# Gate products in four groups of 32 output partitions, and one normalisation moved from VectorE to GpSimd, in a one-core decoder kernel

## The chip, the cores and the metric

The kernel runs on one core of a Trainium2 chip. Its time is the device time of one launch in microseconds (us). Three runs of the kernel before gave 1087.9, 1089.44 and 1091.88 us; their median, 1089.44 us, is what a change is held against.

Engines are named as in the profile: PE is TensorE (PEld its weight loads), DVE is VectorE, ACT is ScalarE, POOL is GpSimd, SP issues most DMAs. They run side by side and meet at semaphores.

## The reference

On x of 8 sequences x 256 tokens x 1024 features (2048 tokens, D = 1024), all in float32:

```
x = x + attn(layernorm(x))            # embedding to 128 features, 4 layers of long convolution and MLP, back to 1024
x = x + xattn(layernorm(x), ctx)      # see below
x = x + ffn(layernorm(x))             # 8 experts of 1024x1024, top 2 per token, softmax of the two gate logits
```

In `xattn` every (sequence, feature) keeps the tokens whose context value is among the largest 154 of 256 (`crucial`) and has the others as a second set. Of both sets the maximum and mean over the tokens go through a 7-tap convolution over the features, a normalisation over all of them and a sigmoid; this gate multiplies the features of the set. In `ffn` the logits are `layernorm(x) @ gate_w` with `gate_w` of 1024 x 8; they choose each token's two experts.

## The kernel before

Everything is in one program for one core, written engine by engine, with semaphores by hand; nothing is scheduled by a tool. X holds the tokens as 16 tiles of 128 tokens x 1024 features; T holds the same data turned, as 8 blocks of 128 features x 2048 tokens; M holds the mask of crucial tokens in bfloat16. The stages that matter here, with their places in the profiled execution:

- **Up to 376 us**: the 4 layers, and on the side the masks from the context.
- **Stage A, 376 to 464 us**: one step per tile t. PE adds the last product of the attention part (`products`, L243 to L246) for tile t + 3. DVE takes mean and variance of tile t (`ln_stats`, L226 to L231). POOL raises the variance to the power -1/2 (`ln_pow`, L235, one 128x1 instruction per tile). DVE writes the normalised tile, (x - mean) * rstd, into one of two buffers, `ring` (`normed`, L1806, a tensor_scalar of 128x1024). PE turns it (L1569), ACT copies it into T and sums it (L1701). Three tiles later DVE multiplies T with the mask and takes the maximum (`crucial`, L1789, four instructions of 128x256 per tile), one tile after that it takes the rest and its maximum (`maxima`, L1798, four as well); ACT sums the crucial part (L1710). DVE's own program gives the order: statistics of t, `crucial` of t - 3, `normed` of t, `maxima` of t - 4.
- **Gate products, first part.** The logits are linear in x, so the part of normalised x is taken from T ahead of the gating: `first_part(c, first, last)` (L1333) multiplies gate_w with 512 tokens, 8 products of 128x8 weights and 512 columns for each of 4 chunks c, all summed into partitions 0 to 7 of one bank. PE does five halves (4 products each) behind the last tiles of stage A, two halves in stage B, the last one in stage C.
- **Stage B, 464 to 477 us**: the convolution on PE (L1590 to L1595), and a chain between DVE, PE, POOL and ACT for the normalisation and the sigmoid. PE fills its waits with `keep_busy` (L1603), six dense bfloat16 products each time, whose results nobody reads.
- **Stage C, 477 to 530 us**: one step per sequence b. DVE and POOL multiply T by the gate (`gated_half`, L1472), PE turns it back (L1621), DVE adds it to X (L1877) and takes new statistics. `second_part` (L1640) multiplies gate_w with the gated T: 8 products with 256 columns per sequence. The 8-partition sums are copied by DVE (L1897, L1905) and turned by PE (L1628, L1647: transposes of 8 partitions).
- **530 to 564 us**: DVE routes the tokens. **From 564 us**: the experts, 37 tiles of 16 products each, PE alone (L2099).

Of the kernel before, what the change touches and what calls it, by code (L numbers as in the profile page):

```python
# [31 lines left out]
def crucial_count(c):  # L32
    f = int(LAMBDA * c // 1)
    return f + f % 2


def decoder_kernel(nc, x, ctx_map, w_in, b_in, ln1_w, ln1_b, phz_re, phz_im, lc_re, lc_im, sc_lin, ln2_w, ln2_b,
# [33 lines left out]
    with ctx:  # L71
# [3 lines left out]
        def sem(name):  # L75
            return ctx.enter_context(nc.semaphore(name))
# [21 lines left out]
        wout_t, bout_b = late[:, 0:D], late[:, D:2 * D]  # L98
        gate = sb("gate", [P, KD, E])
        convw = sb("convw", [P, 2 * TAPS])  # L100
# [47 lines left out]
        ld_misc = sem("ld_misc")  # L148
        ld_gate = sem("ld_gate")
        const_ready = sem("const_ready")  # L150
        set_pe = sem("set_pe")
# [230 lines left out]
        with nc.Block() as block:  # L382
            @block.sync
            def _(sp):
# [49 lines left out]
                context(3)  # L434
                sp.dma_start(gate[:, :, :], gate_w.rearrange("(k p) e -> p k e", p=P)).then_inc(ld_gate, 16)
                weights(2)
# [12 lines left out]
            def _(pool):  # L449
# [73 lines left out]
                def last_threshold(b):  # L523
# [784 lines left out]
        pooled = ewide[:, 0:4 * KD * B].rearrange("p (m i k b) -> p m i k b", m=2, i=2, k=KD)  # L1308
        logits = sb("logits", [P, NT, E])
        totals = logits[:, :, :].rearrange("p t e -> p (t e)")[:, 0:KD * B].rearrange("p (k b) -> p k b", k=KD)  # L1310
# [12 lines left out]
        def pool_at(i, n):  # L1323
            b, h = divmod(n, CT)
            return pooled[:, 0, i, h * KU:(h + 1) * KU, b]

        def first_part(pe, c, first, last):

            if first == 0:
                pe.wait_ge(t_set, (c + 1) * KD * GROUP // S)  # L1330
                pe.wait_ge(x1_done, 2 * (NT - 2) + c + 1)
            for k in range(first, last):
                mm = nc.tensor.matmul(bank[P1_SUMS[c]][0:E, :], gate[:, k, :], T[:, k, c * GROUP:(c + 1) * GROUP], start=(k == 0), stop=(k == KD - 1))  # L1333
            if last == KD:
                mm.then_inc(p1_mm, 1)
# [22 lines left out]
        std = in_late(NT)  # L1358
        g_part = in_late(E)
        known = in_late(NT, E)  # L1360
        shift = in_late(NT, E)
# [95 lines left out]
        P1 = N // GROUP  # L1457
        by_expert = [fin[0:E, u, :] for u in range(2)]

# [29 lines left out]
        col_s = [sb(f"col_s{u}", [P, QK], U32) for u in range(IN_FLIGHT)]  # L1489
        col_d = [sb(f"col_d{u}", [P, 1], U32) for u in range(IN_FLIGHT)]  # L1490
        col_p = [sb(f"col_p{u}", [P, 1]) for u in range(IN_FLIGHT)]
        xg_in = [sem(f"xg_in{u}") for u in range(IN_FLIGHT)]
# [10 lines left out]
        with nc.Block() as block:  # L1503
# [22 lines left out]
            def _(pool):  # L1526
                for t in range(CT, NT):
                    ln_pow(pool, 0, t)

# [30 lines left out]
            def _(pe):  # L1560
# [63 lines left out]
                def first_turned(c):  # L1624
                    pe.wait_ge(p1_cp, c + 1)
                    for u in range(GROUP // P):
                        t = c * (GROUP // P) + u
                        mm = nc.tensor.transpose(bank[P1_BANK][:, t * E:(t + 1) * E], by_expert[c % 2][:, u * P:(u + 1) * P], ident[0:E, 0:E])  # L1628
                    mm.then_inc(p1_tp, 1)

                def second_part(b):
# [7 lines left out]
                    for k in range(KD):  # L1639
                        mm = nc.tensor.matmul(bank[P2_SUMS[b % 2]][0:E, 0:S], gate[:, k, :], T[:, k, b * S:(b + 1) * S], start=(k == 0), stop=(k == KD - 1))  # L1640
                    mm.then_inc(p1_mm, 1)

                def second_turned(b):
                    pe.wait_ge(p1_cp, P1 + b + 1)
                    for h in range(CT):
                        t = CT * b + h
                        mm = nc.tensor.transpose(bank[P2_BANK][:, t * E:(t + 1) * E], by_expert[b % 2][:, h * P:(h + 1) * P], ident[0:E, 0:E])  # L1647
                    mm.then_inc(l_mm, 1)
# [131 lines left out]
            def _(dve):  # L1780
# [20 lines left out]

                def normed(t):
                    if t >= 2:
                        hold(dve, x1_tp, (t - 1) * KU)
                    dve.wait_ge(ln_rstd, t + 1)
                    v.tensor_scalar(ring[t % 2], X[:, t, :], mean_of(0, t), rstd_of(0, t), ALU.subtract, ALU.mult).then_inc(ln_out, 1)  # L1806

                for t in range(NT + LAG + 1):
# [40 lines left out]
                link(v.tensor_scalar(z[:, :, :], z[:, :, :], 0.0, None, ALU.max))  # L1849
                link(v.tensor_reduce(g_part, gate[:, :, :].rearrange("p k e -> p e k"), AX.X, ALU.add))  # L1850
                dve.wait_ge(g_act, 1)
# [41 lines left out]
                def first_sums(c):  # L1893
                    if c >= 2:
                        hold(dve, p1_tp, c - 1)
                    hold(dve, p1_mm, c + 1)
                    v.tensor_copy(by_expert[c % 2], bank[P1_SUMS[c]][0:E, :]).then_inc(p1_cp, 1)  # L1897

                def second_sums(b):
# [4 lines left out]
                    hold(dve, p1_mm, P1 + b + 1)  # L1904
                    v.tensor_copy(by_expert[b % 2][:, 0:S], bank[P2_SUMS[b % 2]][0:E, 0:S]).then_inc(p1_cp, 1)  # L1905

# [315 lines left out]
```

## Time and profile before

| | |
|---|---|
| runs | 1087.9, 1089.44, 1091.88 us; median 1089.44 |
| profiled execution | 1089.82 us, of which the span of the instructions is 1087.9 us |
| busy, whole span | PE 92%, DVE 50%, POOL 42%, ACT 35% |
| mean granted clock of PE | 0.955 of 2.4 GHz |
| L2099, the experts | 511.1 us of PE |
| L1333 and L1640, the gate products | 30.1 and 28.8 us of PE |

The span is what lies between the first and the last instruction of the program. A busy time is the union of the instructions of a group; a mean is over single ones. PE's records overlap, since a product starts while the one ahead of it drains: what a product costs in a series is the distance of two starts. PE writes two records for each float32 product (64 records for the 32 products of L1333). A number in square brackets behind a row is the idle time of that engine just ahead of it and what ended it. Idle time of an engine that others do not wait for costs nothing.

### The profile page before, as it was taken

To read this page: it belongs to the slowest core of one execution; us is meant where nothing else is said; L and a number is where in the kernel's file an instruction comes from. 1 tells how busy PE (TensorE), PEld (TensorE's weight loads), DVE (VectorE), ACT (ScalarE), POOL (GpSimd) and SP (SyncE) were. 2 spreads that over 40 slices of the span, in tenths; PEclk is the share of its full clock that TensorE was granted. 3 is DMA by queue.
4 is the path that set the end of the run, shared out by engine and by line. 5 is a ranking of instruction groups with operands and counts; after the bars stand their busy time and mean duration, and the time that the engine had idled before them with its cause. 6 is when DMAs were issued, how large, how long until landed. Compare 5 with 4: busy or idle time off the path is not lost. (4 is left out here: it accounts for less than half of the span.)

```text
span 1087.9 us, 13206 instructions
## 1 busy us (share of the span) xinstructions
PE 995.9 (92%) x3505; PEld 525.7 (48%) x3512; DVE 538.7 (50%) x1547; ACT 383.5 (35%) x1032; POOL 453.9 (42%) x567
## 2 busy tenths in 40 slices
PE   6888989999989799899469999999999999999995
PEld 5777555565555454245234444444444444444442
DVE  5645878999978889979952111111211111111111
ACT  2344868888865278668410000000000000000000
POOL 4823655665552010048244334333334444444441
PEclk9888989999989899899759999999999999999998
DMA  7320120110001330007758463737337364373332
GB/s 298 129 98 2 50 88 1 59 40 2 1 1 54 144 113 1 2 20 286 295 208 259 103 203 77 231 77 226 82 82 226 77 204 104 77 231 77 77 77 39
DMA packets 38461, 120.24 MB, mean 111 GB/s; under 512 B 6220, under 2 KB 9351, under 8 KB 38408
## 3 DMA queue, kind: packets, MB, share of 16 engines
q1 hardware_dynamic: 25592, 79.77, 19.8%
q0 software_dynamic: 12816, 39.86, 16.7%
q8 instruction: 21, 0.34, 0.1%
q14 instruction: 32, 0.26, 0.1%
HBM read 82.91 MB, written 36.70 MB: 110 GB/s over the span
## 5 line engine op out<-in xcount | busy, mean ns | idle before, releaser
L2099 PE MATMUL bank<-T,X 128*128 x1184 | 511.1, 595 | 3.7 <-issue 3.7
L2099 PEld LDWEIGHTS bank<-T,X 128*128 128x128 f32 x1184 | 225.9, 191 | 288.3 <-issue 288.3
L2144 DVE TENSOR_SCALAR X<-bank,col_p 128x512 f32<-128x512 f32 x37 | 27.8, 751 | 397.1 <-PE bank L2099 397.1
L2117 ACT ACTIVATE X<-bank,col_p 128x512 f32<-128x512 f32 x37 | 25.4, 687 | 495.8 <-PE bank L2099 469.7
L2062 POOL DMA_INDIRECT out_dram<-X,col_d x37 | 60.0, 1622 | 264.3 <-DVE X L2144 248.1
L2053 POOL DMA_INDIRECT X<-x_nrm,col_s x152 | 145.5, 957 | 50.8 <-issue 46.2
L850 ACT ACTIVATE M<-X,T 128x256 bf16<-128x256 f32 x152 | 75.0, 500 | 0.0
L490 POOL TENSOR_TENSOR rs<-ve,neg_half 128x4 f32<-128x4 f32 x36 | 43.7, 1214 | 57.9 <-DVE ve L978 57.9
L665 PE MATMUL bank<-nat,T 128*128 128x512 f32 x128 | 63.2, 614 | 2.5 <-ACT X L838 1.4
L1501 DVE STREAM_TRANSPOSE X<-X 128x1024 f32<-128x1024 f32 x39 | 48.4, 1240 | 26.3 <-DMA X<-x_nrm,col_s 12.7
L673 PE MATMUL bank<-X,T 128*128 128x512 f32 x128 | 60.6, 602 | 0.0
L607 PE MATMUL bank<-ident,rs 128*128 128x128 f32 x320 | 44.5, 285 | 16.4 <-POOL rs L490 14.2
L607 PEld LDWEIGHTS bank<-ident,rs 128*128 128x128 f32 x320 | 41.7, 195 | 36.5 <-POOL rs L490 23.0
L235 POOL TENSOR_TENSOR late<-late,neg_half 128x1 f32<-128x1 f32 x32 | 17.7, 556 | 93.3 <-DVE late L231 93.0
L838 ACT ACTIVATE X<-bank,T 128x512 f32<-128x512 f32 x64 | 43.5, 686 | 19.4 <-PE bank L665 17.9
L1009 DVE MAX8 T<-T 128x8 f32<-128x256 f32 x128 | 44.8, 412 | 0.1
L984 DVE TENSOR_TENSOR nat<-H,bank 128x512 f32<-128x512 f32 x36 | 24.5, 682 | 38.9 <-PE bank L607 38.5
L969 DVE TENSOR_TENSOR_SCAN X<-layer_par,X 128x256 f32<-128x256 f32 x64 | 42.7, 730 | 2.1 <-POOL X L494 2.0
L481 POOL TENSOR_TENSOR T<-T 128x8 f32<-128x8 f32 x88 | 38.2, 434 | 7.9 <-POOL T L481 1.4
L665 PEld LDWEIGHTS bank<-nat,T 128*128 128x128 f32 x128 | 21.7, 191 | 36.4 <-ACT X L838 21.8
L602 PEld LDWEIGHTS bank<-inv_col,nat 128*128 128x128 f32 x288 | 37.2, 202 | 2.6 <-ACT nat L825 2.2
L602 PE MATMUL bank<-inv_col,nat 128*128 128x1 f32 x288 | 37.1, 250 | 0.8 <-ACT nat L825 0.8
(341 smaller groups left out, 1426.6 us busy)
## 6 DMA issues: line engine op xcount, KB each, us to landing
T<-in_L_ffn_expert_w_dram SPq DMA_DIRECT2D x8, 4096.0 KB, 17.6
out_dram<-X SPq DMA_DIRECT2D x17, 512.0 KB
M<-in_x_dram SPq DMA_DIRECT2D x16, 512.0 KB, 7.2
X<-in_x_dram SPq DMA_DIRECT2D x16, 512.0 KB, 5.9
x_nrm<-H SPq DMA_DIRECT2D x16, 512.0 KB, 3.4
T<-in_ctx_dram SPq DMA_DIRECT2D x9, 512.0 KB, 3.7
X<-x_nrm,col_s POOLq DMA_INDIRECT x152
X<-in_ctx_dram SPq DMA_DIRECT2D x4, 512.0 KB, 7.0
```

The source lines that it names most:

```text
L490: g.tensor_tensor(rs[:, v % CH, :], ve[:, v % CH, :], neg_half[:, 0:TPC], ALU.pow).then_inc(done, 1)
L602: mm = nc.tensor.matmul(var_at(v, first)[:, i:i + 1], chunk(sq, v)[:, i * P:(i + 1) * P], inv_col[:, :], start=True, stop=True)
L607: mm = nc.tensor.matmul(bank[to][:, i * P:(i + 1) * P], rs[:, v % CH, i:i + 1].to_broadcast([P, P]), ident[:, :], start=True, stop=True)
L665: nc.tensor.matmul(bank[HD[t % 2]][:, :], w1s[v // CH % 2][:, t * P:(t + 1) * P], chunk(yn, v), start=True, stop=True).then_inc(hid_mm, 1)
L673: mm = nc.tensor.matmul(h_bank(v), w2c[v // CH % 2][:, t, :], hid[:, v % 2, t, :], start=False, stop=(t == FT - 1), skip_group_check=True)
L838: a.activation(hid[:, v % 2, t, :], bank[HD[t % 2]][:, :], ACT.Silu, bias=b1f[v // CH % 2][:, t:t + 1]).then_inc(hid_act, 1)
L850: a.activation(out_, tile_y(b, i), ACT.Sign, bias=at[b % 2][:, i:i + 1], accum_out=sums[b % 2][:, i:i + 1]).then_inc(done, 1)
L1009: v_.max(top16[b % 2][:, h * HT + i, r * 8:(r + 1) * 8], w[:, h, i, :]).then_inc(round_max, 1)
L1501: nc.vector.transpose(xgt_blocks[u], xg_blocks[u]).then_inc(xg_tp, 1)
L2053: g.indirect_dma_start(out=xg[u][:, c * QD:(c + 1) * QD], out_offset=None, in_=x_quarters, in_offset=bass.IndirectOffsetOnAxis(ap=col_s[u] ...
L2062: g.indirect_dma_start(out=out[:, :], out_offset=bass.IndirectOffsetOnAxis(ap=col_d[u][:, 0:1], axis=0), in_=yv[u], in_offset=None, comput ...
L2099: mm = nc.tensor.matmul(bank[2 * u + n][:, :], xgt[u][:, k, :], Tf[:, ds(odd * D + (k * N + n * BANK), BANK)], start=(k == 0), stop=(k == ...
```

## The change

- The weights `gate` get 32 columns per block instead of 8; POOL clears them first (one memset of 128x256 at the start of its program), and the DMA of gate_w, which now waits for that, fills columns 0 to 7.
- The 8 products of a sum no longer go to the same 8 partitions. Product k writes 32 partitions beginning at 32 * (k mod 4), so that the four groups each sum two products. The sums are copied by DVE with all 128 partitions.
- The transposes of the 8-partition sums become products with `sum_e`, a 128x8 matrix of ones and zeros that turns the sums and adds up the four groups at once. DVE makes `sum_e` from the identity with one tensor_reduce in stage B.
- `normed` leaves DVE's program and stands in POOL's, for every tile behind the power of that tile.
- `logits`, `col_d` and `col_p` get no memory of their own and share that of `center`, `mv` and `ve`, which are free by then.

```
+        gate = sb("gate", [P, KD, GROUP_E])                       # GROUPS = 4, GROUP_E = 32
+        sp.wait_ge(gate_clear, 1)
+        sp.dma_start(gate[:, :, 0:E], ...)
+        g.memset(gate[:, :, :], 0.0).then_inc(gate_clear, 1)
...
+        def of_group(sums, k):
+            j = k % GROUPS
+            return sums[j * GROUP_E:(j + 1) * GROUP_E, :]
...
-                mm = nc.tensor.matmul(bank[P1_SUMS[c]][0:E, :], gate[:, k, :], T[...], start=(k == 0), stop=(k == KD - 1))
+                mm = nc.tensor.matmul(of_group(bank[P1_SUMS[c]], k), gate[:, k, :], T[...], start=(k < GROUPS), stop=(k >= KD - GROUPS))
...
-        mm = nc.tensor.transpose(bank[P1_BANK][...], by_expert[c % 2][:, u * P:(u + 1) * P], ident[0:E, 0:E])
+        mm = nc.tensor.matmul(bank[P1_BANK][...], by_expert[c % 2][:, u * P:(u + 1) * P], sum_e[:, :], start=True, stop=True)
...
 POOL
-                for t in range(CT, NT):
-                    ln_pow(pool, 0, t)
+                def normed(t):
+                    if t >= 2:
+                        pool.wait_ge(x1_tp, (t - 1) * KU)
+                    pool.wait_ge(ln_rstd, t + 1)
+                    nc.gpsimd.tensor_scalar(ring[t % 2], X[:, t, :], mean_of(0, t), rstd_of(0, t), ALU.subtract, ALU.mult).then_inc(ln_out, 1)
+                for t in range(NT):
+                    if t >= CT:
+                        ln_pow(pool, 0, t)
+                    normed(t)
 DVE
-                    if t < NT:
-                        normed(t)
...
+                v.tensor_reduce(sum_e[:, :], ident[...].rearrange("p (j e) -> p e j", j=GROUPS)[:, 0:E, :], AX.X, ALU.add)
...
-                    v.tensor_copy(by_expert[c % 2], bank[P1_SUMS[c]][0:E, :]).then_inc(p1_cp, 1)
+                    v.tensor_copy(by_expert[c % 2], bank[P1_SUMS[c]][:, :]).then_inc(p1_cp, 1)
```

DVE's program in the middle of stage A, before: what stands between the last `crucial` instruction of a tile (the first row) and the first `maxima` instruction (ISA is how the program lists these two kinds; the rows with ewide alone read their result).

```order
L1789 ISA H,ewide<-T,M 128x256
L1789 ISA ewide 128x1
L1806 TENSOR_SCALAR nat<-X,late 128x1024
L1798 ISA fin,ewide<-T,H 128x256
L1798 ISA ewide 128x1
```

The same place of DVE's program now (the line numbers have moved by 21).

```order
L1810 ISA H,ewide<-T,M 128x256
L1810 ISA ewide 128x1
L1819 ISA fin,ewide<-T,H 128x256
L1819 ISA ewide 128x1
L1819 ISA fin,ewide<-T,H 128x256
```

One instruction per tile is gone there, and the eight of `crucial` and `maxima` stand in one row. POOL's program at the start of stage A, before (L235 is the power, x14 says how many stand in a row):

```order
L1525 UNCONDITIONAL_BRANCH
L235 TENSOR_TENSOR late<-late,neg_half 128x1 x14
L1531 TENSOR_TENSOR late<-late,neg_half 128x2
L1472 TENSOR_TENSOR T<-T,nat 128x4x256 x4
```

and now:

```order
L1538 UNCONDITIONAL_BRANCH
L1544 TENSOR_SCALAR nat<-X,late 128x1024 x2
L240 TENSOR_TENSOR late<-late,neg_half 128x1
L1544 TENSOR_SCALAR nat<-X,late 128x1024
L240 TENSOR_TENSOR late<-late,neg_half 128x1
```

The sixteen instructions of 128x1024 stand on POOL, each behind the power of its tile. On PE the order of the products is what it was; only their output partitions and, for 24 small ones, their kind differ.

## Rows read from the trace of the kernel before

**Rows 1.** The chain that ended last, in order of time: start, length, what
```profile
563.64 511.13 PE bank L2099 x1184
```

**Rows 2.** Busy time by stretch: length, each engine (instructions), clock, DMA share, GB/s
```profile
394.00:464.00 70.00, 63.48 (x215) 27.75 (x216) 65.11 (x283) 53.62 (x242) 5.40 (x10) 0.95 0.02 9
...
477.00:530.00 53.00, 50.77 (x299) 28.36 (x298) 48.34 (x124) 44.58 (x76) 42.05 (x35) 1.00 0.60 229
```

**Rows 3.** Timeline of DVE, one tile of stage A: start, length, instruction
```profile
410.66 0.43 DVE L1789 CUSTOM_DVE_ANT_0 H<-T,M 128x256 f32<-128x256 f32 x1 [0.23 <-ACT T L1701]
...
412.05 0.81 DVE L1806 TENSOR_SCALAR nat<-X,late 128x1024 f32<-128x1024 f32 x1
412.77 0.42 DVE L1798 CUSTOM_DVE_ANT_0 fin<-T,H 128x256 f32<-128x256 f32 x1
...
416.21 0.43 DVE L1789 CUSTOM_DVE_ANT_0 H<-T,M 128x256 f32<-128x256 f32 x1 [0.23 <-issue]
```

**Rows 4.** Timelines of DVE and PE: where the steady pace begins; PE's own pace
```profile
394.00 0.42 DVE L1789 CUSTOM_DVE_ANT_0 H<-T,M 128x256 f32<-128x256 f32 x1 [1.25 <-ACT late L1710]
413.68 1.13 PE L1569 MATMUL bank<-ident,nat 128*128 128x128 f32 x8
...
418.51 1.05 PE L1569 MATMUL bank<-ident,nat 128*128 128x128 f32 x8
```

**Rows 5.** Timeline of POOL: the power of a tile, beside DVE and alone
```profile
387.50 0.75 POOL L235 TENSOR_TENSOR late<-late,neg_half 128x1 f32<-128x1 f32 x1 [3.57 <-DVE late L231]
410.50 0.54 POOL L235 TENSOR_TENSOR late<-late,neg_half 128x1 f32<-128x1 f32 x1 [5.01 <-DVE late L231]
```

**Rows 6.** Timelines of POOL and DVE: L974 beside a long POOL instruction, and without
```profile
95.14 1.35 POOL L494 TENSOR_TENSOR X<-nat,T 128x512 f32<-128x512 f32 x1 [10.86 <-ACT nat L830]
95.28 1.76 DVE L974 TENSOR_TENSOR X<-X,T 128x512 f32<-128x512 f32 x1
260.61 0.68 DVE L974 TENSOR_TENSOR X<-X,T 128x512 f32<-128x512 f32 x1
```

**Rows 7.** POOL's groups by shape: names, shapes, count | busy, mean ns | idle before
```profile
L548 POOL TENSOR_SCALAR_AFFINE_SELECT upto_neg<-upto_neg 128x128 f32<-128x128 f32 x1 | 0.3, 286 | 0.0
L550 POOL TENSOR_SCALAR_AFFINE_SELECT ewide<-ewide 128x390 f32<-128x390 f32 x1 | 0.5, 501 | 0.0
L1472 POOL TENSOR_TENSOR T<-T,nat 128x1024 f32<-128x1024 f32 x14 | 32.8, 2363 | 6.0 <-ACT nat L1739 6.0
```

**Rows 8.** Timeline of PE, end of stage A and stage B
```profile
440.80 1.97 PE L1569 MATMUL bank<-ident,nat 128*128 128x128 f32 x8 [4.58 <-DVE nat L1806]
...
453.56 10.47 PE L1333 MATMUL bank<-T,gate 128*8 128x512 f32 x24
464.87 0.71 PE L1590 MATMUL bank<-ewide,band 128*128 128x128 f32 x4 [0.84 <-DVE ewide L1826]
...
467.15 1.46 PE L1603 MATMUL bank<-ones,ident 128*128 128x512 bf16 x6
...
470.34 7.03 PE L1333 MATMUL bank<-T,gate 128*8 128x512 f32 x16
```

**Rows 9.** Busy time by stretch around PE's pause of 4.58 us
```profile
436.00:439.00 3.00, 0.22 (x2) 0.00 (x0) 2.55 (x11) 1.21 (x7) 0.54 (x1) 1.00 0.00 0
442.00:445.00 3.00, 3.00 (x7) 0.74 (x6) 2.59 (x11) 3.00 (x17) 0.54 (x1) 0.50 0.01 3
448.00:464.00 16.00, 16.00 (x49) 4.41 (x48) 14.85 (x77) 10.69 (x49) 0.54 (x1) 1.00 0.01 2
```

**Rows 10.** Timeline of PE: keep_busy products ahead of the experts, at the low clock
```profile
549.97 1.87 PE L1603 MATMUL bank<-ones,ident 128*128 128x512 bf16 x4
```

**Rows 11.** Timelines of DVE and PE in stage C: sums of chunks 2, 3, of sequences 0, 1
```profile
484.41 1.28 DVE L1897 COPY fin<-bank 8x512 f32<-8x512 f32 x2
486.08 7.07 PE L1640 MATMUL bank<-T,gate 128*8 128x256 f32 x32
489.85 0.41 DVE L1905 COPY fin<-bank 8x256 f32<-8x256 f32 x1 [1.53 <-PE bank L1640]
```

More of the change, by code:

```diff
@@ L1332, in first_part @@
             for k in range(first, last):
-                mm = nc.tensor.matmul(bank[P1_SUMS[c]][0:E, :], gate[:, k, :], T[:, k, c * GROUP:(c + 1) * GROUP], start=(k == 0), stop=(k == KD - 1))
+                mm = nc.tensor.matmul(of_group(bank[P1_SUMS[c]], k), gate[:, k, :], T[:, k, c * GROUP:(c + 1) * GROUP], start=(k < GROUPS), stop=(k >= KD - GROUPS))
             if last == KD:
@@ L1359, in decoder_kernel @@
         g_part = in_late(E)
+        sum_e = in_late(E)
         known = in_late(NT, E)
@@ L1457, in decoder_kernel @@
         P1 = N // GROUP
-        by_expert = [fin[0:E, u, :] for u in range(2)]
+        by_expert = [fin[:, u, :] for u in range(2)]
         def expert_src(e):
@@ L1489, in decoder_kernel @@
         col_s = [sb(f"col_s{u}", [P, QK], U32) for u in range(IN_FLIGHT)]
-        col_d = [sb(f"col_d{u}", [P, 1], U32) for u in range(IN_FLIGHT)]
-        col_p = [sb(f"col_p{u}", [P, 1]) for u in range(IN_FLIGHT)]
+        col_d = [mv[:, u, 0:1].bitcast(U32) for u in range(IN_FLIGHT)]
+        col_p = [ve[:, u, 0:1] for u in range(IN_FLIGHT)]
         xg_in = [sem(f"xg_in{u}") for u in range(IN_FLIGHT)]
@@ L1627, in first_turned @@
                         t = c * (GROUP // P) + u
-                        mm = nc.tensor.transpose(bank[P1_BANK][:, t * E:(t + 1) * E], by_expert[c % 2][:, u * P:(u + 1) * P], ident[0:E, 0:E])
+                        mm = nc.tensor.matmul(bank[P1_BANK][:, t * E:(t + 1) * E], by_expert[c % 2][:, u * P:(u + 1) * P], sum_e[:, :], start=True, stop=True)
                     mm.then_inc(p1_tp, 1)
@@ L1639, in second_part @@
                     for k in range(KD):
-                        mm = nc.tensor.matmul(bank[P2_SUMS[b % 2]][0:E, 0:S], gate[:, k, :], T[:, k, b * S:(b + 1) * S], start=(k == 0), stop=(k == KD - 1))
+                        mm = nc.tensor.matmul(of_group(bank[P2_SUMS[b % 2]], k)[:, 0:S], gate[:, k, :], T[:, k, b * S:(b + 1) * S], start=(k < GROUPS), stop=(k >= KD - GROUPS))
                     mm.then_inc(p1_mm, 1)
@@ L1646, in second_turned @@
                         t = CT * b + h
-                        mm = nc.tensor.transpose(bank[P2_BANK][:, t * E:(t + 1) * E], by_expert[b % 2][:, h * P:(h + 1) * P], ident[0:E, 0:E])
+                        mm = nc.tensor.matmul(bank[P2_BANK][:, t * E:(t + 1) * E], by_expert[b % 2][:, h * P:(h + 1) * P], sum_e[:, :], start=True, stop=True)
                     mm.then_inc(l_mm, 1)
@@ L1800, in maxima @@
                     ins.then_inc(re_max, 1)
[L1802 to L1806, printed above, removed]
                 for t in range(NT + LAG + 1):
```

13 lines of the change are left out of this document (8 added, 5 removed).

## The prediction

> **What bounds the kernel now.** I read the chain of waits first: it is 511.13 us of the experts' products on PE from 563.64 us to the end, without a pause, and the change does not touch them [rows 1]. So the question is only when PE can begin with them, and I read the busy times by stretch for the stages ahead. In stage A DVE is busy 65.11 of 70 us, in stage C 48.34 of 53 [rows 2]; PE's 63.48 and 50.77 look larger, but its records overlap. The timeline of DVE shows a fixed pace: `crucial` of one tile starts at 410.66, of the next at 416.21, that is 5.55 us per tile, with one gap of 0.23 us [rows 3]. The pace begins at 394.00, where DVE stops waiting for ACT (1.25 us) [rows 4]. So stage A is DVE's from 394.00 to its end at 464. Stage B is a chain that passes through PE. In stage C the reader is to look for DVE waiting for PE: it does so once, 1.53 us, for the sums of sequence 0 [rows 11]. The gate products are 59 us of PE, but in stages A and C PE is not what is waited for.
>
> **Term 1: `normed` leaves DVE.** In the tile shown it takes 412.77 - 412.05 = 0.72 us of DVE's time [rows 3]. There are 16. Numbers 0 to 4 stand ahead of the wait at 394.00, which ACT's sums and PE's products set: what DVE saves there, it waits longer. The other 11 count: 11 x 0.72 = 7.9 us, if POOL's work costs DVE nothing. PE and ACT could follow: without a wait PE's transposes of two tiles start 418.51 - 413.68 = 4.83 us apart [rows 4], and DVE would need 5.55 - 0.72 = 4.83.
>
> But POOL's work is not free for DVE. `crucial` and `maxima` both read two tensors from SBUF. The power on POOL takes 0.54 us alone and 0.75 us when it starts 0.07 us behind such a DVE instruction [rows 5]: POOL waited 0.2 us. The other way round, DVE's L974, also with two inputs from SBUF, takes 0.68 us and took 1.76 us when a POOL instruction of 1.35 us had started 0.14 us ahead of it [rows 6]: it lost 1.08 us, until 0.13 us before POOL's record ended. So I let the two exclude each other, instruction by instruction.
>
> How long is POOL's tensor_scalar of 128x1024? No row shows it. One-input instructions take 286 ns for 128 and 501 ns for 390 elements: 0.82 ns per element and 0.18 us, which gives 1.02 us for 1024 [rows 7]. The lower bound of its cost to DVE is nothing; the upper one is the two-input product of the same size, 2.36 us [rows 7]. I take 1.02, the row nearest in kind (one input).
>
> When does it fall? The power starts at 410.50 and ends at 411.04 [rows 5]; `normed` can start at 411.12, while DVE is in the second of its four `crucial` instructions (four from 410.66 to 412.05, one every 0.35 us) [rows 3]. POOL waits some 0.2 us, as the power did, gets in before the third, and its record ends at 411.12 + 1.02 + 0.2 = 412.34. DVE's third instruction, due at 411.35, starts 0.15 us before that, at 412.19: it loses 0.84 us and saves 0.72. That is +0.12 us per tile, in every tile, since the power always starts behind the statistics and `crucial` stands right behind them. Ten tiles: +1.2. Tile 5 meets DVE's wait at 394.00, loses only about 0.3 and saves 0.72: -0.4. The first two tiles are turned about 0.2 us later. Queued behind DVE's late instruction are `maxima`, the next statistics and so the next power, which all move with it; PE gets its tile no later than now (412.34 against 412.05 + 0.81 = 412.86). **Term 1: +1.0 us, with -7.9 (no exclusion) and +14 (2.36 us on POOL: 2.2 lost, 0.72 saved, ten times) as bounds.** Each 0.1 us on POOL is 1 us of the kernel.
>
> The Trainium skill (GPSIMD Engine Reference, 3.1) puts an elementwise body of up to two operations at 1.03 cycles of 1.2 GHz per element, an estimate of 0.88 us for 1024, without what starts and ends it. By that alone the term would be -0.4 us. No run here shows this instruction.
>
> **Term 2: the gate products.** A product with 512 columns costs 10.47 us / 12 = 0.87 us, in two records [rows 8]. Four groups may run beside each other: the factor lies between 1 and 4. The two records of one product go to the same partitions, so I let only the neighbours of different groups overlap and take 2. Then the 12 products behind stage A's last transposes take 5.2 us instead of 10.47, and PE, now busy until DVE ends the stage (464.04), is idle from about 459 on; DVE's last results come at 464.87 plus term 1. That is a pause of 7 us. A pause of 4.58 us was followed by the lower clock, 0.50 (1.2 GHz) at 442 to 445, and 1.00 again from 448 on, 7 us after work had resumed at 440.80 [rows 8, 9]. So stage B begins at 1.2 GHz. The convolution takes 467.15 - 464.87 = 2.28 us [rows 8] and as many more: +2.2. Of the first `keep_busy`, six records of 0.24 us, each costs 0.47 at the low clock [rows 8, 10], which is 1.3 us more if the clock is still low, and behind the second one a little. Its return is somewhere between 3 and 7 us after the start, so I take half: +0.8. **Stage B: +3.0 us, bounds 0 (the clock stays) and +4.5.** The 8 products behind it (7.03 us now) end at 3.5 instead and wait for the gate; DVE's gating, not PE, sets back(0).
>
> In stage C the wait of 1.53 us for L1640 [rows 11] goes in part: the sums of chunks 2 and 3 are copied from 484.41 to 485.69 [rows 11]; the eight small products that turn them are sixteen records with 128-column weights now, and eight such records take 1.05 us [rows 4], so from about 485.1, when chunk 2 is there, to 487.1; sequence 0's eight products take a quarter of 7.07 us: 488.9 instead of 489.85. **Stage C: -1.0 us, bounds -1.53 and +0.5** (should the clock be low there too). Behind it DVE has no wait for PE to lose, and its work is as before: the copies have more partitions, not more columns. What is late next is DVE itself. At the end the routing and the DMA of the normalised rows both hang on stage C and move with it.
>
> Other edits: the memset stands at the start of POOL's program, where the work waits for loads; the reduce for `sum_e` lies beside ACT's sigmoid; shared memory costs no time. 0.
>
> **Sum**: +1.0 + 3.0 - 1.0 = +3.0 us on the profiled execution's 1089.82, 1092.8. The median of the runs is 0.4 us below that execution: **1092.4 us**.
>
> The Trainium skill (TensorE: Matmul & The Clock Gate, Part 3) gives 2.38 times the speed for three groups of output columns, and says that products end in the order in which they start. By 2.38 or more the wait in stage C goes wholly, and the sum would be 0.5 us less. This trace has no such groups.
>
> **Rivals.**
> - *POOL and DVE do not exclude each other here* (`crucial` is another kind of instruction than L974, or POOL finds room only beside the statistics, which read one tensor). Then term 1 is -7.9 and the sum -5.9: 1083.5. For it: the power that ran from 410.50 to 411.04 held up none of DVE's instructions beside it, which stayed 0.35 us apart [rows 3, 5]; but it reads one element. Against: the 0.2 us of the other power [rows 5] was lost to this very instruction.
> - *POOL's instruction is slower than 1.02 us*, with two per-partition operands instead of constants: the other side. At 1.7 us, half way to the bound, it is +6.8 more: 1099. From 1.25 us on (+5.4 in all) the kernel is measurably slower.
> - *The clock holds, or the groups do not overlap*: no pause, so stage B costs nothing; the sum is +1.0 or 0: 1090.
> - *The exclusion is worse than counted*: POOL's instruction keeps DVE out for all of its length each time and the power too, +2: 1094.5. This lies in my own case's range.
>
> **Numbers.** My case 40%, with 1089.5 to 1096 as its own range; no exclusion 22%; slow POOL 20%; clock or groups 18%. A measurement of this kernel can tell about 0.5% (5.4 us) from no change: faster is below 1084.0, slower above 1094.9. Faster: 16 of the 22 and 4 from the edges of the others, 20%. Slower: 18 of the 20 and 10 of my case, 28%. Within: 52%. The range for 8 in 10 reaches to the first rival on one side and past the 1.7 us case on the other: 1083 to 1100.
>
> **What would show it.** In the profile after: POOL's tensor_scalar near 1.0 us, and every third `crucial` instruction of a tile longer by some 0.8 us; starts of `crucial` 5.67 us apart (4.83 if there is no exclusion). Records of L1333 in pairs, 24 of them in 5 us; the clock at 0.50 when the convolution starts, and L1590 to L1603 in 4.4 us. L1905 waiting 0.5 us for sequence 0. The experts unchanged at 511 us. I am wrong if stage A gets shorter by more than 3 us, if stage B keeps its length, or if PE's experts change.

## The result, and the profile after

| | before | after |
|---|---|---|
| median of the runs | 1089.44 us (5 runs, 1087.9 to 1092.13) | 1100.24 us (5 runs, 1097.72 to 1101.49) |
| ratio | | 1.0096, 95% interval 1.0078 to 1.0114 |
| span of the profiled execution | 1087.9 us | 1099.1 us |
| busy: PE, DVE, POOL | 92%, 50%, 42% | 89%, 49%, 47% |

The kernel became slower, by 1%: +10.5 us by the ratio, where I had +3.0. Line numbers of the kernel after are higher: `normed` is L1544 on POOL, the power L240, `crucial` L1810, `maxima` L1819, the transposes L1590, `first_part` L1345, the convolution L1611 to L1616, `keep_busy` L1624, the experts L2113.

I cut each profile at four points: the last product ahead of stage A (PE, 370.93 us before and 372.10 after), the first product of the convolution, the first gated half on DVE, and the first product of the experts; "the end" is that of the last DMA issue on POOL, about 10 us ahead of the end of the span. Lengths in us:

| | stage A | stage B | stage C and routing | experts to the end |
|---|---|---|---|---|
| before | 93.95 | 9.99 | 88.78 | 514.39 |
| after | 102.50 | 13.10 | 87.27 | 514.10 |
| difference | +8.55 | +3.11 | -1.51 | -0.29 |
| forecast | +1.0 | +3.0 | -1.0 | 0 |

The first point lies 1.17 us later in this profile already, ahead of everything that the change touches but the memset at the start; the other profiles below scatter from 368.95 to 373.79 there, so I put it down to the run and compare lengths. How far a single length scatters can be read from the probe kernel below, whose stages A to C are those of the kernel before: it has 93.58, 9.99 and 89.27 us, that is -0.37, 0.00 and +0.49. Differences of up to half a microsecond in stages A and C are therefore not told from nothing.

So one term is off, that of stage A. The page after shows why in one row of its costliest groups (count, busy us, mean ns):

```profile
L2113 PE MATMUL bank<-T,X 128*128 x1184 | 510.8, 594 | 3.7 <-issue 3.7
...
L1544 POOL TENSOR_SCALAR nat<-X,late 128x1024 f32<-128x1024 f32 x16 | 66.6, 4163 | 4.6 <-POOLq L1253 1.9
```

POOL's instruction takes 4.16 us on average, four times the 1.02 us that I took from [rows 7], and more than my upper bound of 2.36. The start of stage A, from the timelines of POOL, PE and DVE (start, length, instruction, idle time and what ended it):

```profile
377.76 7.59 POOL L1544 TENSOR_SCALAR nat<-X,late 128x1024 f32<-128x1024 f32 x2 [1.88 <-POOLq L1253]
381.62 1.97 PE L1590 MATMUL bank<-ident,nat 128*128 128x128 f32 x8 [9.26 <-POOL nat L1544]
387.90 0.42 DVE L1810 CUSTOM_DVE_ANT_0 H<-T,M 128x256 f32<-128x256 f32 x1 [6.43 <-ACT T L1722]
400.78 0.43 DVE L1810 CUSTOM_DVE_ANT_0 H<-T,M 128x256 f32<-128x256 f32 x1 [4.59 <-ACT late L1731]
```

PE waits 9.26 us for the first normalised tile (6.29 before), and DVE, which has ended the statistics and has nothing but `crucial` to do, waits 6.43 and 4.59 us for what comes of it, ahead of tiles 0 and 2. Then the pace is DVE's again. One tile of the middle, POOL and DVE:

```profile
411.87 4.36 POOL L1544 TENSOR_SCALAR nat<-X,late 128x1024 f32<-128x1024 f32 x1 [0.18 <-PE bank L1590]
412.66 1.25 DVE L1819 CUSTOM_DVE_ANT_0 fin<-T,H 128x256 f32<-128x256 f32 x1
413.84 0.08 DVE L1819 DVE_READ_ACCUMULATOR2_ANT ewide<- 128x1 f32 x1
413.84 0.41 DVE L1819 CUSTOM_DVE_ANT_0 fin<-T,H 128x256 f32<-128x256 f32 x1
416.93 0.43 DVE L1810 CUSTOM_DVE_ANT_0 H<-T,M 128x256 f32<-128x256 f32 x1 [0.23 <-issue]
```

The tile before had begun `crucial` at 411.27, so the pace is 5.66 us (5.55 in [rows 3]; I had 5.67). One DVE instruction takes 1.25 instead of 0.42 us: 0.83 lost against 0.72 saved. But POOL works until 416.23, and the three instructions of `maxima` behind it run at 0.35 us beside it. At the end of the stage:

```profile
462.02 1.97 PE L1590 MATMUL bank<-ident,nat 128*128 128x128 f32 x8 [3.04 <-POOL nat L1544]
466.19 0.42 DVE L1810 CUSTOM_DVE_ANT_0 H<-T,M 128x256 f32<-128x256 f32 x1 [2.46 <-ACT late L1731]
```

The eight transposes of 462.02 take 1.97 us where [rows 4] have 1.05: the clock was 0.50, which makes about 0.9 us of this lateness, an estimate from the two durations.

From the first point to `crucial` of tile 3 it takes 33.51 us, before 28.62: +4.89. The nine tiles from there take 51.40, before 50.10: +1.30. From `crucial` of tile 12 to the convolution, 17.60 and 15.22: +2.38. Together 8.57.

Stage B, PE's timeline, its clock in a stretch of the convolution (length, each engine (instructions), clock), and the first gated half, after and then before:

```profile
463.92 4.41 PE L1345 MATMUL bank<-T,gate 128*32 128x512 f32 x24
474.61 1.22 PE L1611 MATMUL bank<-ewide,band 128*128 128x128 f32 x4 [6.28 <-DVE ewide L1839]
...
478.92 2.44 PE L1624 MATMUL bank<-ones,ident 128*128 128x512 bf16 x6
...
483.09 1.92 PE L1345 MATMUL bank<-T,gate 128*32 128x512 f32 x16
...
475.00:478.00 3.00, 3.00 (x16) 3.00 (x16) 0.00 (x0) 0.00 (x0) 0.00 (x0) 0.50 0.00 0
...
487.71 2.36 DVE L1485 TENSOR_TENSOR T<-T,nat 128x1024 f32<-128x1024 f32 x2 [0.28 <-DVE nat L1922]
```

```profile
474.86 2.36 DVE L1472 TENSOR_TENSOR T<-T,nat 128x1024 f32<-128x1024 f32 x2 [0.28 <-DVE nat L1908]
```

A pause of 6.28 us, the clock at 0.50, the convolution in 4.31 us instead of 2.28 [rows 8], the first `keep_busy` in 2.44 instead of 1.46: as forecast. The gate products are faster than I had them: 16 records in 1.92 us at clock 1.00, where [rows 8] has 7.03. The 24 records at the end of stage A took 4.41 us, with the clock at 0.50 from 464 to 467 us; at the pace of the 16 they would take 2.9, an estimate.

### The profile page after: what moved, and what is told of

The parts are those of the page before. It is cut to its first block and busy times, and to the rows that moved or that the text cites. A ratio compares the mean times of both kernels' runs of the same rounds, so it can differ in the third digit from the quotient of the medians.

```text
span 1099.1 us, 13272 instructions
## 1 busy us (share of the span) xinstructions
PE 974.4 (89%) x3537; PEld 528.2 (48%) x3544; DVE 535.1 (49%) x1532; ACT 384.1 (35%) x1032; POOL 521.5 (47%) x584
## 5 line engine op out<-in xcount | busy, mean ns | idle before, releaser
L2113 PE MATMUL bank<-T,X 128*128 x1184 | 510.8, 594 | 3.7 <-issue 3.7
L2113 PEld LDWEIGHTS bank<-T,X 128*128 128x128 f32 x1184 | 225.8, 191 | 288.2 <-issue 288.2
L2158 DVE TENSOR_SCALAR X<-bank,ve 128x512 f32<-128x512 f32 x37 | 27.8, 751 | 394.7 <-PE bank L2113 394.7
L2131 ACT ACTIVATE X<-bank,ve 128x512 f32<-128x512 f32 x37 | 25.4, 687 | 495.2 <-PE bank L2113 469.7
L2076 POOL DMA_INDIRECT out_dram<-X,mv x37 | 60.0, 1622 | 263.6 <-DVE X L2158 175.0
L1544 POOL TENSOR_SCALAR nat<-X,late 128x1024 f32<-128x1024 f32 x16 | 66.6, 4163 | 4.6 <-POOLq L1253 1.9
L1590 PE MATMUL bank<-ident,nat 128*128 128x128 f32 x128 | 20.9, 315 | 24.8 <-POOL nat L1544 24.8
```

Of the source, the lines that this page charges most:

```text
L1544: nc.gpsimd.tensor_scalar(ring[t % 2], X[:, t, :], mean_of(0, t), rstd_of(0, t), ALU.subtract, ALU.mult).then_inc(ln_out, 1)
L2076: g.indirect_dma_start(out=out[:, :], out_offset=bass.IndirectOffsetOnAxis(ap=col_d[u][:, 0:1], axis=0), in_=yv[u], in_offset=None, comput ...
L2113: mm = nc.tensor.matmul(bank[2 * u + n][:, :], xgt[u][:, k, :], Tf[:, ds(odd * D + (k * N + n * BANK), BANK)], start=(k == 0), stop=(k == ...
```

## The experiments

All ratios are to the kernel before, run beside each kernel, with 95% intervals. Line numbers differ by a few from kernel to kernel. Lengths by the same four points, as differences to before in us:

| kernel | ratio | stage A | B | C and routing |
|---|---|---|---|---|
| the change | 1.0096 (1.0078 to 1.0114) | +8.55 | +3.11 | -1.51 |
| POOL only | 1.0077 (1.0061 to 1.0093) | +8.31 | +0.09 | +0.21 |
| groups only | 1.0033 (1.0019 to 1.0047) | -0.07 | +3.93 | -0.25 |
| groups, filled | 0.9990 (0.9974 to 1.0005) | -0.38 | 0.00 | -0.35 |
| POOL phased | 1.0029 (1.0014 to 1.0045) | +2.97 | 0.00 | -0.20 |
| POOL not phased | 1.0024 (1.0011 to 1.0038) | +2.94 | 0.00 | -0.19 |
| groups, filled to C | 1.0039 (1.0023 to 1.0055) | -0.37 | 0.00 | +3.50 |
| filled to C, phased | 1.0067 (1.0050 to 1.0085) | +3.14 | 0.00 | +3.74 |
| every other tile | 0.9967 (0.9951 to 0.9982) | -1.94 | 0.00 | +0.55 |
| every other, groups, filled | 0.9958 (0.9941 to 0.9975) | -1.92 | 0.00 | -1.65 |
| a copy on POOL | 1.0029 (1.0013 to 1.0044) | +0.45 | +3.51 | -1.00 |
| two groups | 1.0030 (1.0013 to 1.0047) | -0.41 | +3.75 | -0.29 |

### The parts apart: POOL alone, groups alone

POOL alone: the kernel before with the change's edit of `normed`, nothing else.

> The kernel before with normed on POOL and nothing else: gate products and their sums as before. Theory (the parts add up): the whole of stage A's loss in the changed kernel, 9.7 us between the starts of the convolution (464.87 and 474.61), is POOL's, so stage A is 9 to 11 us longer here too, stage B and C are as before, the clock at the convolution is 1.00, and the median is 1099 us. Rival (the two parts make each other worse: the short gate products leave PE idle, the clock falls, and the transposes behind it are late): stage A is only some 6 us longer, 1095 us.

1.0077, stage A +8.31 us, stages B and C as before; the median was 1097.89 us. The parts add up in the profile (8.31 and 8.55 in stage A), and the rival's 6 us is out. Still the 9 to 11 us that I expected are missed: I had counted between absolute places in the two profiles, and 1.17 of those 9.7 us lie ahead of stage A.

Groups alone:

```
-                    normed(t)                      # on POOL, behind the power of t
+                    if t < NT:                     # on DVE, behind crucial(t - LAG), as before
+                        normed(t)
```

> The changed kernel with normed back on VectorE, as before: only the gate products in four groups, with sum_e and the shared memory. Theory: stage A as before (conv starts at 464.9), a PE pause of 7 us ahead of the convolution, the clock 0.50 there, stage B 3.1 us longer (as in the changed kernel), stage C and routing 1.5 us shorter: 1091 us. Rival (the groups cost nothing by themselves; the low clock of stage B came from POOL's late tiles): stage B as before, 1088 us.

1.0033, 1093.16 us where I expected 1091: stage A as before, stage B +3.93 (I had 3.1; the first `keep_busy` takes 2.77 us here, 2.44 in the changed kernel), and stage C only 0.25 shorter instead of 1.5, for which see the end of this part. PE's timeline and clock:

```profile
452.95 4.48 PE L1345 MATMUL bank<-T,gate 128*32 128x512 f32 x24
464.89 1.22 PE L1603 MATMUL bank<-ewide,band 128*128 128x128 f32 x4 [7.46 <-DVE ewide L1839]
...
469.20 2.77 PE L1616 MATMUL bank<-ones,ident 128*128 128x512 bf16 x6
...
465.00:468.00 3.00, 3.00 (x15) 3.00 (x15) 0.00 (x0) 0.00 (x0) 0.00 (x0) 0.50 0.00 0
```

Stage C differs by the clock as well. DVE waits there for the sums of sequence 0 (1.53 us before, [rows 11]). In the changed kernel this wait is 0.14 us; in the groups alone 1.08, and 0.97 in the next kernel, which has the groups and `normed` on DVE too. PE's products of sequences 0 and 1 in the changed kernel, then the same products and DVE's copy in the next kernel:

```profile
500.08 1.93 PE L1661 MATMUL bank<-T,gate 128*32 128x256 f32 x32
```

```profile
488.10 3.41 PE L1655 MATMUL bank<-T,gate 128*32 128x256 f32 x32
490.21 0.42 DVE L1921 COPY fin<-bank 128x256 f32<-128x256 f32 x1 [0.97 <-PE bank L1655]
```

The granted clock was 1.00 from 500 to 502 us in the first and 0.50 from 488 to 491 in the second. So the groups take away nearly all of this wait where the clock is up at this place, and a third of it where it is not. Why it is up in one kernel and not in the other is not shown.

### Is stage B the clock?

```
                 first_part(pe, c, part * KU, (part + 1) * KU)      # the five halves of stage A
+                pe.wait_ge(x1_done, 2 * NT)
+                keep_busy(5, 12)
```

> As the groups alone, with 12 dense bfloat16 products behind each of the five halves of gate products in stage A (60 in all, about the time that the groups save there), whose results nobody reads. Theory (the 3 us of stage B are the clock, and the clock falls for PE's pause): the clock is 1.00 at the convolution, L1611 to the first keep_busy takes 3.7 us as before instead of 6.7, stage A is not longer, and the median is 3 us below the groups alone: 1088 us. Rival (stage B's length comes from the products themselves or from sum_e on DVE): no change against the groups alone, 1091 us. Third: the filler makes transposes late: stage A longer by 2 us or more.

0.9990; its median is 3.4 us below that of the groups alone, and stage B, whose work is the same, is 3.93 us shorter:

```profile
465.76 0.71 PE L1612 MATMUL bank<-ewide,band 128*128 128x128 f32 x4 [0.40 <-DVE ewide L1841]
...
468.04 1.46 PE L1579 MATMUL bank<-ones,ident 128*128 128x512 bf16 x6
...
465.00:468.00 3.00, 2.60 (x22) 2.24 (x21) 0.52 (x3) 0.09 (x1) 0.00 (x0) 1.00 0.00 0
```

The same products take 2.28 us at 1.00 and 4.31 at 0.50; what differs is what PE did ahead of them, the 60 added products and a pause of 0.40 us against one of 7.46. That stage B's cost is the clock is shown, and that useless products buy it back. The ratio's interval includes 1, so a gain over the kernel before is not shown.

### What POOL's instruction costs, by itself

Nine instructions on POOL ahead of the kernel's work, each waiting for the one ahead; then the same nine beside 64 DVE products of 128x256.

```
+ shapes: g.tensor_scalar(dst, src, a1, b1, subtract, mult) for 1024, 512, 256 elements; with constants for 1024, 512;
+         one operation (mult) with an operand, with a constant; g.tensor_tensor(dst, src, src, mult); g.tensor_copy(dst, src)
+ DVE:    64 x v.tensor_tensor(band[...256], H[:, 0:256], H[:, 256:512], mult)
```

> The kernel before, with nine POOL instructions ahead of its first work, twice: alone, and beside a row of 64 DVE products of 128x256 with two inputs from SBUF. Its own time says nothing; the durations are read. tensor_scalar with two per-partition operands took 3.79 us for 1024 elements in the changed kernel. Theory A (time per element, for the per-partition operands): 128x512 takes 1.9 to 2.0 us, 128x256 1.0, with constants 1024 take 1.0 us. Theory B (a fixed price of about 2.8 us per instruction for those operands): 128x512 takes 3.3 us, 128x256 3.0. Theory C (two operations cost it, whatever the operands): constants take 3.8 too, and one operation some 2. Beside the DVE row: by my prediction's rule DVE stands still for all of each POOL instruction; by the changed kernel's trace, where one DVE instruction in a tile lost 0.83 us and POOL's took 4.37 instead of 3.79, DVE stands still for 0.8 us in each.

POOL alone:

```profile
2.63 3.80 POOL L552 TENSOR_SCALAR H<-H 128x1024 f32<-128x1024 f32 x1
6.53 2.09 POOL L553 TENSOR_SCALAR H<-H 128x512 f32<-128x512 f32 x1
8.72 1.22 POOL L554 TENSOR_SCALAR H<-H 128x256 f32<-128x256 f32 x1
10.03 3.63 POOL L555 TENSOR_SCALAR H<-H 128x1024 f32<-128x1024 f32 x1
...
15.76 2.85 POOL L557 TENSOR_SCALAR H<-H 128x1024 f32<-128x1024 f32 x1
18.70 2.77 POOL L558 TENSOR_SCALAR H<-H 128x1024 f32<-128x1024 f32 x1
21.55 1.89 POOL L559 TENSOR_TENSOR H<-H 128x1024 f32<-128x1024 f32 x1
23.50 1.04 POOL L560 COPY H<-H 128x1024 f32<-128x1024 f32 x1
```

Time per element: (3.80 - 1.22) / 768 = 3.4 ns, and 0.4 us besides, so theory B falls. The operands cost 0.17 us (3.80 against 3.63), so A has the right form and the wrong cause. The second operation costs 0.86 us (3.63 against 2.77), and one operation with a constant still takes 2.77, more than a product of two tensors (1.89) and 2.7 times a copy: C is nearest, but low. It is tensor_scalar itself that is slow here; the other one-input instructions, from which I took 0.82 ns per element, say nothing of it. The Trainium skill (GPSIMD Engine Reference, 3.1) has 1.03 cycles of 1.2 GHz per element for up to two operations, an estimate of 0.88 us; this case's trace disagrees by a factor of 4, and only the copy's 1.04 us comes near.

Beside the DVE row, POOL's first two and the DVE group (shortest/median/longest ns):

```profile
24.82 4.51 POOL L552 TENSOR_SCALAR H<-H 128x1024 f32<-128x1024 f32 x1
29.43 19.64 POOL L553 TENSOR_SCALAR H<-H 128x512 f32<-128x512 f32 x1
...
L1147 DVE TENSOR_TENSOR band<-H x64: 410/412/1255, 24.7 to 46.7; 128x256 f32<-128x256 f32 x64
```

One DVE instruction of the 64 took 1.255 us, the others 0.41: POOL's instruction of 1024 elements held DVE up for 0.84 us (from 25.75 us on) and worked on for some 2.7 us beside it, after it had itself waited 0.71 us (4.51 instead of 3.80). The next one, of 512, did not get in at all while DVE's row lasted and took 19.64 us instead of 2.09. Why the first got in and the second did not is not shown, and the other seven ran after the row had ended. The Trainium skill (SBUF — State Buffer, "Summary: rules for kernel authors") says that when a DVE instruction has two inputs in SBUF and the GpSimd one reads SBUF, the one that issues second is blocked until the first has finished. This trace agrees that each keeps the other out, but here POOL's instruction did so for 0.84 of its 3.8 us.

### Put the hold beside the statistics

```
+                    if 4 <= t <= 14:                       # POOL; DVE writes 0 to 3 and 15
...
+                        pool.wait_ge(ln_out, t)
+                        pool.wait_ge(re_max, t - LAG)      # phased only: maxima(t - 4) is done, DVE begins statistics
+                        nc.gpsimd.tensor_scalar(ring[t % 2], X[:, t, :], ...)
```

> The kernel before (gate products untouched); POOL writes normed for tiles 4 to 14 only, VectorE for 0 to 3 and 15, and POOL begins each one only when DVE has ended maxima of tile t-4, that is when DVE begins the statistics of the next tile. Theory: POOL's tensor_scalar holds DVE's two-input instructions for 0.84 us once, at its beginning (one instruction of 1.25 instead of 0.42 us in each tile of the changed kernel, 1.25 in the probe), and not the one-input statistics; then nothing is lost, DVE needs 5.55 - 0.72 = 4.83 us per tile, POOL 4.5, and stage A is 6 to 8 us shorter: 1082.5 us, ratio 0.994. Rival: POOL's 3.8 us of latency, a tile later than VectorE's, makes ACT's copies and so crucial late, the pace stays near 5.5 us: 1089 to 1091 us.

> As the phased kernel, with the same tiles on POOL, but without the wait for maxima: POOL starts as soon as the power is there, beside crucial. Theory: in each tile DVE saves 0.72 us and loses 0.83 us, +0.1 us per tile as in the changed kernel's steady part (5.66 against 5.55 us), and no late start: stage A 1 us longer, 1090.5 us. Rival (the phase does not matter, only the late first and last tiles did): as fast as the phased kernel, 1083 us.

1.0029 and 1.0024, 1092.76 and 1092.84 us: the gain is missed, and both are above every forecast. The hold went as expected: in the phased kernel's timeline none of the 128 `crucial` and `maxima` instructions is longer than 0.43 us. But DVE waits for ACT in every second tile (timelines of POOL and DVE, then DVE's waits in all of stage A: us, times, longest):

```profile
429.82 3.79 POOL L1534 TENSOR_SCALAR nat<-X,late 128x1024 f32<-128x1024 f32 x1 [1.53 <-DVE ewide L1804]
...
426.76 0.43 DVE L1795 CUSTOM_DVE_ANT_0 H<-T,M 128x256 f32<-128x256 f32 x1 [1.39 <-ACT late L1716]
...
431.59 0.42 DVE L1795 CUSTOM_DVE_ANT_0 H<-T,M 128x256 f32<-128x256 f32 x1 [0.23 <-issue]
...
DVE H L1795 <- ACT late L1716: 13.8, 7, 5.0
```

Starts of `crucial` are 4.83 and 6.0 us apart in turn: it needs the copies of both tiles of a sequence, and the second comes later than before. At the end `crucial` of tile 14 stood at 460.01 (456.46 before), 5.0 us of wait. Without the phase the pace is the 5.66 of the theory, but tile 14 is late in the same way (5.6 us behind tile 13 instead of 3.0), which I had not counted. So the two are equal for different reasons, and the phase by itself is not tested by their times, only by their rows.

Only even tiles, the first of each sequence, on POOL, and the odd one written by DVE after `maxima`:

```
+        ON_POOL = (4, 6, 8, 10, 12)
+                    if t - 1 in ON_POOL:               # DVE, after maxima(t - LAG - 1), waiting for ln_out >= t
+                        normed(t)
```

> The kernel before, with only tiles 4, 6, 8, 10 and 12 normalised by POOL, each begun when maxima of four tiles ahead is done; VectorE writes all the others, and the one behind a POOL tile only after maxima. Theory (what cost the phased kernel its gain is that crucial of an even tile needs the copies of the odd one behind it, and that one came from POOL too late: DVE waited 1.4 us for it every second tile and 5.0 us at the end): the even tile has two steps of slack, DVE waits for nothing, saves 0.72 us five times, stage A is 3.6 us shorter, 1086 us, ratio 0.9967. Rival: the later transposes push PE's products and ACT's copies so that DVE waits all the same: no faster than before, 1089 us or more.

> The same five tiles on POOL, on top of the gate products in groups with the fillers in stage A. Theory: adds up, 3.6 us below the filled groups kernel, ratio to before 0.9957, 1085 us. Rival: the fillers, whose length is that of the products of before, now end after DVE and set the convolution: 2 us or more of the gain are lost.

0.9967 and 0.9958, the forecast ratios. By the profiles stage A gains 1.9 of the 3.6 us: `crucial` follows `crucial` after 4.83 us in two of five cases; in two others DVE still waits about 1 us, and the first (tile 4) lies ahead of the steady pace:

```profile
413.62 3.79 POOL L1535 TENSOR_SCALAR nat<-X,late 128x1024 f32<-128x1024 f32 x1 [2.67 <-DVE ewide L1805]
...
416.12 0.42 DVE L1796 CUSTOM_DVE_ANT_0 H<-T,M 128x256 f32<-128x256 f32 x1 [0.96 <-ACT late L1717]
```

So the theory holds for the way, and only half for the size, and that the ratios hit is in part luck. The interval of the first, -2.0 to -5.3 us, begins where the 1.9 of stage A ends; its stage C, +0.55, has DVE waiting 2.02 us for a DMA near the end where the kernel before waits 1.30, as the probe kernel has. The second gains 1.3 us more in stage C than the filled groups, which my theory did not have: DVE's wait for the sums of sequence 0 is 0.11 us there. This last kernel has the lowest median, 1084.94 us against 1090.42 beside it, but the intervals do not tell it from the first, 1087.20.

### Fillers in stage C

```
                 first_part(pe, 3, 0, KU)
+                keep_busy(7, 16)
...
+                    for i in range((0, 48)[b] if b < 2 else 24):       # in second_part, ahead of its signal, 256 columns each
+                        mm = nc.tensor.matmul(bank[P2_SUMS[b % 2]][:, S:2 * S], ident..., ones..., start=True, stop=True)
```

> The filled groups kernel with fillers in stages B and C too: 16 dense products of 512 columns ahead of the first transposes back, and behind second_part of each sequence (twice as many for sequence 1, none for 0) 24 products of 256 columns, counted in with the sums, so that PE is as long busy as before the change. Theory (the rest of what the groups cost is the low clock of the transposes back, 2.37 and 3.68 instead of 1.97 us, for which DVE waits 1.0 us): clock 1.00 from 466 to 525, no wait of DVE in stage C, 1 to 1.5 us below the kernel with fillers in stage A only: 1088.3 us, ratio 0.998. Rival: stage C is DVE's, nothing changes: 1089.5.

> Fillers in stages A to C, gate products in groups, and the phased normed on POOL for tiles 4 to 14. Theory: the gains add up, and since the fillers are as long as the products they replace, stage A ends where that of the phased kernel does: 1081.5 us, ratio 0.992. Rival (in the phased kernels PE's 10.5 us behind the last transposes end after DVE and set the convolution): no better than the phased kernel alone, 1083 us or more.

Both forecasts fall: 1.0039, with stage C and routing 3.85 us longer than with fillers in stage A alone. The clock was 1.00 but for one stretch, but that stretch (488 to 491 us) holds the products of sequence 0, 3.48 us long, for which DVE still waits 0.9 us. And the 48 products stood ahead of the transposes of sequence 2, which came at 496.83 us (491.44 with fillers in stage A alone, whose convolution began 0.14 us earlier), and DVE waited for them:

```profile
488.16 3.48 PE L1656 MATMUL bank<-T,gate 128*32 128x256 f32 x32
491.58 5.42 PE L1658 MATMUL bank<-ones,ident 128*128 128x256 bf16 x48
496.83 1.91 PE L1637 MATMUL bank<-ident,T 128*128 128x128 f32 x16
...
DVE X L1896 <- PE bank L1637: 3.3, 1, 3.3
```

So this run does not test the theory that the low clock costs 1 us in stage C. The changed kernel does, as shown above: at clock 1.00 the wait is 0.14 us. The combined kernel adds the same 3.7 us to the phased one's 3: it tells only that the costs add up. Its rival is met in the number and not in its reason.

### Was it the duration alone?

```
-  nc.gpsimd.tensor_scalar(ring[t % 2], X[:, t, :], mean_of(0, t), rstd_of(0, t), ALU.subtract, ALU.mult)
+  nc.gpsimd.tensor_copy(ring[t % 2], X[:, t, :])
```

> The changed kernel, with POOL's tensor_scalar made a copy of the same 128x1024: the subtraction and the multiplication are left out, so that everything behind it works on x that is not normalised; what is read is the time. In the probe this copy took 1.04 us, the 1.02 us that my prediction took for tensor_scalar. Theory (the prediction failed in this duration alone): PE gets its first tiles at once, DVE loses what it saves, and the time is that of the groups alone (1.0033 of before) plus about 1 us: ratio 1.003 to 1.0045, 1093 to 1094.5 us. Rival (the 6 us at the start of stage A and the 2.4 us at its end come from the wait for the power and the order on POOL, not from the 3.8 us): 1098 us or more.

1.0029, stage A +0.45 us instead of +8.55. POOL's copy and DVE's third `crucial` instruction:

```profile
408.48 1.15 POOL L1544 COPY nat<-X 128x1024 f32<-128x1024 f32 x1
...
408.66 1.25 DVE L1810 CUSTOM_DVE_ANT_0 H<-T,M 128x256 f32<-128x256 f32 x1
```

The ratio is at the lower edge of what I expected, and the prediction's picture of a tile is met: POOL 1.15 us long (I had 1.02 and 0.2 of wait), the third instruction of `crucial` longer by 0.83 (0.84), the pace 5.66 (5.67). The wait for the power and the order on POOL are the same as in the changed kernel, so they are not what costs the 8.55 us.

### How far do groups overlap?

The groups alone, with `j = k % 2`, and copies and sums over 64 partitions.

> The groups-only kernel with two groups instead of four: product k goes to partitions 0 to 31 or 32 to 63 (k mod 2), each group sums four products, the copies and sum_e use 64 partitions. Theory (each group is worked on beside the others, and a product in one group only waits for the product ahead of it in the same group): the 8 products of stage B (16 records), 7.03 us with one group and 1.92 us with four, take 3.6 us. This is the factor 2 that my prediction took for four groups; by its reasoning PE's pause ahead of the convolution is 6 us, the clock 0.50 there, and stage B 3 to 4 us longer, as with four groups: ratio 1.003. Rival (a pause of 6 us, or the longer products ahead of it, leave the clock at 1.00): stage B as before, ratio 0.999 to 1.000.

1.0030. PE's timeline:

```profile
453.00 6.83 PE L1345 MATMUL bank<-T,gate 128*32 128x512 f32 x24
464.79 1.22 PE L1603 MATMUL bank<-ewide,band 128*128 128x128 f32 x4 [4.96 <-DVE ewide L1839]
...
474.00 3.63 PE L1345 MATMUL bank<-T,gate 128*32 128x512 f32 x16
```

16 records take 7.03 us with one group, 3.63 with two, 1.92 with four: factors 1.9 and 3.7, all at clock 1.00. The Trainium skill (TensorE: Matmul & The Clock Gate, Part 3) gives 2.38 for three. That lies between, but at the same gain per group four would give 3.2, an estimate from the page's figure, and here they give 3.7. The clock was 0.50 in the convolution behind a pause of 4.96 us too.

## Why the prediction was right or wrong

- **The bound.** The experts took 510.8 us (511.1 before); all that moved lies ahead of them. Right.
- **Term 1, +1.0 us, measured +8.55.** The step that failed is "How long is POOL's tensor_scalar of 128x1024?": 1.02 us from other one-input instructions, and 2.36 as the upper bound from the product; it is 3.79 alone and 4.36 beside DVE. The bound failed because I took a two-input instruction to be the dearest of its size. The copy shows that this duration is all of it: with 1.15 us the stage is longer by 0.45 us, which is within the scatter of one length.
- **"Each 0.1 us on POOL is 1 us of the kernel"** was wrong as well. It rests on DVE standing still for all of POOL's instruction. DVE loses 0.83 us a tile whether POOL works for 1.15 or for 4.36 us. By this rule 3.79 us would have made the term about +29 us. Duration too short and hold too long cancel in part, and that the time still came out near the end of my range is luck. The steady part so came out as forecast (+1.30 for nine tiles, +1.2 for ten), and the loss came where I saw none: the first tiles, for which I had written that PE gets its tile no later than now, and the last.
- **Exclusion.** The first rival (no exclusion, 1083.5) is out. The second (a slow instruction, 1099 at 1.7 us) had the right cause and came closest in time, but by a wrong way: DVE's loss per tile does not grow with POOL's duration. The last one (POOL keeps DVE out for all of its length) is out by the same 0.83 of 4.36 us.
- **Term 2, stage B: +3.0, measured +3.11** and 3.93 by itself; pause, clock and the two terms in it were right (convolution +2.03 for +2.2, first `keep_busy` +0.98 for +0.8). That the clock may be back 3 us after the start is not in [rows 9], which have it at 0.50 for 4.2 us; in the changed kernel it was back for the second `keep_busy`, which takes 1.46 us as before. The factor of 2 for four groups was wrong (3.7), and did not matter in stage B: with two groups it is 3.75 longer. The rivals of a clock that holds and of groups that do not overlap are out.
- **Stage C: -1.0, measured -1.51** in the change. The term was the right one, the wait for L1640: of 1.53 us 0.14 is left, where I had 0.5, since four groups overlap by 3.7 and not by 2. Where the clock is 0.50 at this place 0.97 to 1.08 us are left, and the stage is only 0.25 to 0.35 us shorter; with a copy on POOL 0.69 is left, and it is 1.00 shorter. My bound of +0.5 for a low clock was too high. By the factor 2.38 the sum would have ended at 488.6 us, which leaves 0.3 us of wait and not none, as I wrote there.
- **Sum.** 1092.4 forecast, 1100.24 measured: 0.24 us above the range of 1083 to 1100, and by the ratio, 1099.9 us, just in it. Not within 0.5% but slower, for which I had 28%. None of my three signs of being wrong (stage A shorter, stage B unchanged, other experts) looked at a stage A that is longer than forecast, and so none of them came.

## What to carry to other kernels

Before an instruction moves to another engine, its own duration there has to be read or measured, not taken from a cheaper kind of the same shape; and a long latency hurts where a pipeline fills and drains, even if the steady part hides it. Speeding up an engine that nobody waits for opens pauses, and here pauses of 5 to 7.5 us ahead of a chain that runs through PE were each followed by the half clock in it, 3 to 4 us in all; dense products in the pause gave it back, as long as none of them stands ahead of work that is waited for. Of this change the groups cost 0.3% without fillers and nothing with them (0.9990, no gain shown), and POOL's help gained only for the tiles that have two steps of slack.

## What the runs showed of the hardware

- POOL's tensor_scalar alone, two operations, float32: 0.4 us and 3.4 ns per element (3.80 us for 1024, 1.22 for 256); for 1024 elements one operation takes 2.77 us, a product 1.89, a copy 1.04.
- With 1024 elements it keeps DVE's instructions with two inputs from SBUF out for 0.83 to 0.84 us, at its beginning, once, not for its 3.8 us; a copy of 1.15 us does so for 0.83 us too. DVE's statistics, with one input, took 0.69 and 0.68 us beside it in the phased kernel, as they do alone. In the other direction a gapless row of such two-input DVE instructions kept a POOL instruction of 2.09 us waiting until the row ended: 19.64 us; the POOL instruction ahead of it had got into the same row after 0.71 us.
- Products into 32 output partitions each run beside each other when the partitions differ: 16 records of 512 columns in 7.03, 3.63 and 1.92 us with one, two and four groups (weights of 8 columns with one, of 32 with two and four).
- In the convolution PE's clock was 0.50 behind pauses of 4.96, 6.28 and 7.46 us and 1.00 behind one of 0.40.
